# State-space block and routed experts: a convolution in three half-width products, and a drain in halves

## The reference, cut to what matters

```python
x = L0_attn_x                                       # (16, 512, 128), fp32
xn = layernorm(layernorm(x)) * norm_w + norm_b
x_in, z = split(xn @ in_proj_w.T)                    # 256 inner channels each
x_conv = conv(x_in, conv_w, taps=4, causal) + conv_b # full 256 x 256 x 4
x_act = silu(x_conv)
delta, B, C = x_act @ x_proj_w.T                     # 1 + 16 + 16
h = h * exp(-softplus(delta)) + B * x_act            # scan over 512 tokens
y = (h . C) * silu(z) @ out_proj_w.T + residual
x = x + layernorm(y)                                 # "third" norm
logits = layernorm(x) @ Wr + br                      # "fourth" norm
for e in 16 experts:                                 # top 2 of each token
    out += w_e * (layernorm((silu(x W1) * (x W3)) W2) * gamma + beta)
x = x + layernorm(out)
```

## Time and profile before

| | us |
|---|---|
| median of 3 runs | 971.87 (971.36 to 972.1) |
| the profiled execution, its own time | 974.93 |
| its span, first to last instruction | 973.1 |
| PE busy | 940.0 (97%) |
| DVE busy | 722.8 (74%) |
| ACT busy | 689.5 (71%) |
| POOL busy | 620.4 (64%) |

### The profile page before, as it was taken

The page is one execution under the profiler, slowest core; times in us unless marked ns, Lnnn a source line. Parts: engine busy times, 40 slices in busy tenths (PEclk is TensorE's granted clock), DMA queues, the critical chain, the costliest instruction groups (busy, mean ns, idle before and its releaser), DMA issues.

```text
span 973.1 us, 26657 instructions
## 1 busy us (share of the span) xinstructions
PE 940.0 (97%) x7207; PEld 833.9 (86%) x7207; DVE 722.8 (74%) x2524; ACT 689.5 (71%) x1358; POOL 620.4 (64%) x813
## 2 busy tenths in 40 slices
PE   8999999999999999998879999999999999999994
PEld 5777887788887887887879999999999999999951
DVE  2379999999999998898623767776767677677656
ACT  3777787777778778765115777777777778778536
POOL 2445777777778777775541666666666666566647
PEclk9999999999999999999988999999999999999997
DMA  4001323121111111110865211111111111111075
GB/s 136 12 12 34 93 93 97 58 62 48 55 56 53 53 43 42 42 42 22 324 238 175 87 44 51 49 51 46 49 50 48 47 50 49 42 53 50 18 293 225
DMA packets 54159, 75.25 MB, mean 77 GB/s; under 512 B 11103, under 2 KB 32865, under 8 KB 53376
## 3 DMA queue, kind: packets, MB, share of 16 engines
q1 hardware_dynamic: 42784, 54.87, 18.4%
q0 software_dynamic: 8672, 16.93, 4.8%
q10 hardware_dynamic: 2560, 1.75, 0.6%
HBM read 47.09 MB, written 27.41 MB: 77 GB/s over the span
## 4 chain that ended last, share of the span: by engine, by line
PE 79%; DVE 7%; POOL 6%; issue 5%; DMA 1%; ACT 1%; POOLq 0%; DVEq 0%; SPq 0%; ACTq 0%
PE pA L1886 11%; PE pR L1886 11%; PE pA L1472 11%; PE pB L1894 6%; PE pY L1894 5%; PE pY L1586 4%; PE pB L1498 3%; PE pB L1632 3%; PE pA L1487 3%; PE pY L1622 3%; PE pA L1443 3%; POOL chosen_scratch L656 2%; PE pY L1605 2%; PE pY L1554 2%; PE pR L1570 2%
## 5 line engine op out<-in xcount | busy, mean ns | idle before, releaser
L656 POOL DMA_INDIRECT chosen_scratch<-yo,got_id x143 | 146.8, 1027 | 93.7 <-issue 87.9
L961 ACT ACTIVATE stage<-w_sb 128x1024 f32 x143 | 151.2, 1057 | 55.7 <-issue 55.6
L1358 DVE TENSOR_TENSOR hidT<-pR,sil 128x512 f32<-128x512 f32 x143 | 98.9, 692 | 81.0 <-ACT sil L956 60.8
L595 POOL DMA_INDIRECT slots_scratch<-xrow,send_at x128 | 134.7, 1052 | 35.3 <-issue 31.3
L1886 PE MATMUL pA<-xsT,stage 128*128 128x128 f32 x1144 | 151.3, 275 | 0.4 <-ACT xsT L945 0.4
L1886 PE MATMUL pR<-xsT,stage 128*128 128x128 f32 x1144 | 151.1, 275 | 0.0
L1886 PEld LDWEIGHTS pA<-xsT,stage 128*128 128x128 f32 x1144 | 139.2, 192 | 0.7 <-ACT xsT L945 0.6
L1886 PEld LDWEIGHTS pR<-xsT,stage 128*128 128x128 f32 x1144 | 139.0, 192 | 0.0
L1472 PE MATMUL pA<-xn,taps 128*128 128x512 f32 x256 | 129.8, 594 | 1.0 <-ACT xn L722 1.0
L646 POOL TENSOR_TENSOR ers<-eve,neg_half 128x1 f32<-128x1 f32 x143 | 81.7, 571 | 57.2 <-DVE eve L1370 40.0
L956 ACT ACTIVATE sil<-pA 128x512 f32<-128x512 f32 x143 | 85.3, 596 | 26.5 <-PE pA L1886 21.7
(11 more groups left out here) (198 smaller groups left out, 2102.0 us busy)
## 6 DMA issues: line engine op xcount, KB each, us to landing
got<-slots_scratch SPq DMA_DIRECT2D x143, 65.0 KB, 1.9
w_sb<-chosen_scratch SPq DMA_DIRECT2D x16, 512.0 KB, 5.4
w_sb<-in_w_dram SPq DMA_DIRECT2D x1, 6144.0 KB
xin<-in_x_dram SPq DMA_DIRECT2D x16, 256.0 KB
xr<-in_x_dram SPq DMA_DIRECT2D x16, 256.0 KB, 3.1
x_scratch<-x SPq DMA_DIRECT2D x16, 256.0 KB
w_sb<-in_w_dram SPq DMA_DIRECT2D x4, 1024.0 KB, 7.2
fx<-x_scratch SPq DMA_DIRECT2D x1, 4096.0 KB
```

What stands on the lines that cost most here:

```text
L595: eng.indirect_dma_start(slots_d, bass.IndirectOffsetOnAxis(ap=send_at[:, s % 2, k, t:t + 1], axis=0), xrow[:, s % 2, k, t, :], None).then ...
L656: eng.indirect_dma_start(chosen_d, bass.IndirectOffsetOnAxis(ap=got_id[:, j % NGOT:j % NGOT + 1], axis=0), yo[:, q, :], None, bounds_check ...
L961: eng.activation(stage[:, j % NSTAGE, :, :].rearrange("p k f -> p (k f)"), w13_sb[:, bass.ds(e, 1), :, :].rearrange("p o k f -> p (o k f)" ...
L1358: eng.tensor_tensor(hidT[:, p, :], pR[:, p, :], sil[:, p, :], ALU.mult).then_inc(hid_ready, 1)
```

## The change

- The second 128 channels of the convolution (f = 1) are made by `fast_conv`: even and odd tokens share a product. Three products of 256 columns, each a sum of two weights, take the place of one of 512 columns with four: six matmuls of 256 columns for four of 512. Their inputs are every other column of `xn` and of its differences `xd` (POOL's new `differ`). `tapx` holds the sums and negatives of taps, made by DVE at the start. ACT copies the shared product (`shared_copy`, 256 columns), and DVE adds it to both halves (`join_taps`, 512 columns) before ACT's silu. The steps behind it wait for `cv_ready`.
- The epsilon of the third and fourth norm is added on POOL, not on DVE (`var_3` and `var_4` go). `shift_3` goes from every sequence; one operation makes all at the end. The copy of the indices in `choose` goes.
- `tail_at` is made inside the last `positions`. `conv`, `expand`, `fold`, the sends and the rest stand in new orders on all four engines, and loads of x stand one place earlier in SP's queue.
- The last sequence's output projection, norms and router are done in two halves of two tiles, in two banks. POOL sends one row between them and the other six after them, where it sent five ahead of them. The counts of `keep_warm` change.
- In stage 3 the negated mean goes, and the last group is normalised and added by DVE and stored by ACT.
- `load_middle` and `load_last`, which the diff also adds, are called nowhere.

The diff, cut to its core:

```diff
+FAST = (1,)
+SHARED = 256
...
+                for n, f in enumerate(FAST):
+                    even, odd = (taps[:, :, tile(f)].rearrange("p (k o) f -> p k o f", o=2)[:, :, o, :] for o in range(2))
+                    eng.tensor_tensor(tapx[:, n, 0:2, :], even, odd, ALU.add).then_inc(taps_ready, 1)
+                    eng.tensor_scalar(tapx[:, n, 2:4, :], odd, -1.0, None, ALU.mult).then_inc(taps_ready, 1)
...
+            def fast_conv(s, f, k):
+
+                n = FAST.index(f)
+                if k == 0:
+                    if n:
+                        need(eng, shared_ready, s, len(FAST), n)
+                    else:
+                        need(eng, prod_ready, s, 2, 2, ago=1)
+                else:
+                    need(eng, xd_ready, s, 1, 1)
+                half_seq = SEQ // 2
+                for q in range(2):
+                    if k == 0:
+                        out, h, src, at_col = pB[:, 1, SHARED:SHARED + half_seq], tapx[:, n, q, :], xn, 1 + 2 * q
+                    elif k == 1:
+                        out, h, src, at_col = pA[:, f, 0:half_seq], taps[:, 2 * q, tile(f)], xd, 2 * q
+                    else:
+                        out, h, src, at_col = pA[:, f, half_seq:SEQ], tapx[:, n, 2 + q, :], xd, 1 + 2 * q
+                    every_other = src[:, s % 2, at_col:at_col + SEQ].rearrange("p (i o) -> p i o", o=2)[:, :, 0]
+                    i = eng.matmul(out, h, every_other, start=q == 0, stop=q == 1)
+                if k == 0:
+                    i.then_inc(shared_mm, 1)
+                elif k == 2:
                     i.then_inc(cv_mm, 1)
...
+            def join_taps(s, f):
+
+                if s is None:
+                    return
+                n = FAST.index(f)
+                need(eng, cv_mm, s, 2, f + 1)
+                need(eng, shared_ready, s, len(FAST), n + 1)
+                need(eng, u_ready, s, 2, f + 1, ago=1)
+                eng.tensor_tensor(cvs[:, n, :].rearrange("p (i o) -> p i o", o=2), pA[:, f, :].rearrange("p (o i) -> p i o", o=2),
+                                  shared[:, :].rearrange("p (i o) -> p i o", o=1).broadcast_to([P, SEQ // 2, 2]), ALU.add).then_inc(cv_ready, 1)
...
+            def shared_copy(s, f):
+                if s is None:
+                    return
+                n = FAST.index(f)
+                need(eng, shared_mm, s, len(FAST), n + 1)
+                if n:
+                    need(eng, cv_ready, s, len(FAST), n)
+                else:
+                    need(eng, cv_ready, s, len(FAST), len(FAST), ago=1)
+                eng.activation(shared[:, :], pB[:, 1, SHARED:SHARED + SEQ // 2], ACT.Copy).then_inc(shared_ready, 1)
...
+            def differ(s):
+
+                if s is None:
+                    return
+                need(eng, xn_ready, s, 1, 1)
+                need(eng, cv_mm, s, 2, FAST[-1] + 1, ago=2)
+                eng.tensor_tensor(xd[:, s % 2, 0:SEQ + 2], xn[:, s % 2, 0:SEQ + 2], xn[:, s % 2, 1:SEQ + 3], ALU.subtract).then_inc(xd_ready, 1)
...
-                need(eng, moments3, s, 9, 9)
-                eng.tensor_tensor(rs3[:, :], ve3[:, :], neg_half[:, 0:NT4], ALU.pow).then_inc(rstd3, 1)
+                need(eng, moments3, s, 8, 8)
+                eng.tensor_tensor(ve3[:, :], mv3[:, s, :, 1:2].rearrange("p t o -> p (t o)"), eps[:, :], ALU.add).then_inc(rstd3, 1)
+                need(eng, rstd3, s, 2, 1)
+                eng.tensor_tensor(rs3[:, s, :], ve3[:, :], neg_half[:, 0:NT4], ALU.pow).then_inc(rstd3, 1)
...
-                need(eng, choice, s, 6, 4)
-                eng.tensor_copy(topi[:, :, :], topi8[:, :, 0:2].rearrange("p t k -> p k t")).then_inc(choice, 1)
-                need(eng, choice, s, 6, 5)
+                need(eng, choice, s, 5, 4)
                 eng.tensor_tensor(chosen[:, s % 2, :, :, :], iota_es[:, :].rearrange("p (a o e) -> p a o e", a=1, o=1).broadcast_to([P, 2, NT4, NE]),
-                                  topi[:, :, :].rearrange("p k (t o) -> p k t o", o=1).broadcast_to([P, 2, NT4, NE]), ALU.is_equal).then_inc(choice, 1)
...
+                if s == NS - 1:
+                    eng.wait_ge(rank_read, NS)
+                    eng.tensor_scalar(tail_at[:, :], running[:, :], slot_no[:, 0:1], None, ALU.add).then_inc(tail_ready, 1)
...
+            def rstd_half(moments, mv, ve, rs, done, h):
+                c = slice(2 * h, 2 * h + 2)
+                eng.wait_ge(moments, 8 * L + 4 + 4 * h)
+                eng.tensor_tensor(ve[:, c], mv[:, c, 1:2].rearrange("p t o -> p (t o)"), eps[:, c], ALU.add).then_inc(done, 1)
+                eng.wait_ge(done, 2 * (L + h) + 1)
+                eng.tensor_tensor(rs[:, c], ve[:, c], neg_half[:, c], ALU.pow).then_inc(done, 1)
...
+            address(L - 1)
+            send_ready(L - 1)
+            send_one(L - 1, 0, 0)
+            rstd_3_half(0)
+            rstd_3_half(1)
+            send_one(L - 1, 0, 1)
+            rstd_4_half(0)
+            rstd_4_half(1)
+            send(L - 1, 1)
+            send(L - 1, 2)
+            send(L - 1, 3)
+            token(L)
...
+            def attend_half(h):
+                eng.wait_ge(xr_loaded, 16 * NS)
+                eng.wait_ge(op_mm, L + 1 + h)
+                for t in half_tiles(h):
+                    i = eng.scalar_tensor_tensor(out=at[:, t, :], in0=xr[:, t, :], scalar=rs1[:, L, t:t + 1], in1=half_bank(h)[:, in_bank(t)], op0=ALU.mult, op1=ALU.add)
+                i.then_inc(at_ready, 1)
...
+            attend_half(0)
+            stats_half(at, at_ready, stats3, moments3, 0)
+            attend_half(1)
+            aggr_3_half(0)
+            stats_half(at, at_ready, stats3, moments3, 1)
+            aggr_3_half(1)
+            residual_half(0)
+            stats_half(x1, x1_ready, stats4, moments4, 0)
+            residual_half(1)
+            aggr_4_half(0)
+            stats_half(x1, x1_ready, stats4, moments4, 1)
+            aggr_4_half(1)
+            shift_4_half(0)
+            shift_4_half(1)
+            eng.scalar_tensor_tensor(out=shift3[:, :, :].rearrange("p s t -> p (s t)"), in0=mv3[:, :, :, 0:1].rearrange("p s t o -> p (s t o)"), scalar=-1.0,
+                                     in1=rs3[:, :, :].rearrange("p s t -> p (s t)"), op0=ALU.mult, op1=ALU.mult).then_inc(shift3_ready, 1)
+            logits_half(0)
+            largest_half(0)
+            where_half(0)
+            logits_half(1)
+            largest_half(1)
+            where_half(1)
+            choose(L)
+            margin(L)
+            positions(L)
...
+                from_state(q[5], 1)
+                bc_turn(q[4], 0)
+                project_gate(q[3], 1)
+                r_turn(q[4], 2)
+                diag_turn(q[4])
+                odd_turn(q[4])
+                x_turn(q[2])
+                project_state(q[3])
+                gram(q[4], 2)
+                gram(q[4], 4)
+                conv(q[2], 0, 0)
+                xf_turn(q[6])
+                delta_turn(q[3])
+                conv(q[2], 0, 1)
+                next_b(q[3])
+                route(q[6])
+                r_turn(q[4], 8)
+                conv(q[2], 0, 2)
+                r_turn(q[4], 4)
+                conv(q[2], 0, 3)
+                r16_turn(q[4], 0)
+                level(q[4], 2)
+                gram(q[4], 8)
+                project_gate(q[2], 0)
+                rank(q[6])
+                r16_turn(q[4], 1)
+                level(q[4], 8)
+                project_out(q[5])
+                level(q[4], 4)
+                states(q[4], 0)
+                conv(q[2], 1, 0)
+                states(q[4], 1)
+                conv(q[2], 1, 1)
+                h_turn(q[4], 0)
+                conv(q[2], 1, 2)
+                h_turn(q[4], 1)
+                from_state(q[4], 0)
...
+            def project_out_half(h):
+                eng.wait_ge(y_step, 11 * NS)
+                if h == 0:
+                    eng.wait_ge(rank_read, L)
+                else:
+                    eng.wait_ge(ht_ready, 2 * NS)
+                for t in half_tiles(h):
+                    for m in range(2):
+                        i = eng.matmul(half_bank(h)[:, in_bank(t)], y[:, m, tile(t)], outproj[:, m, :], start=m == 0, stop=m == 1)
+                i.then_inc(op_mm, 1)
...
             keep_warm(5)
-            project_out(15)
-            keep_warm(46)
-            xf_turn(15)
-            keep_warm(2)
-            route(15)
-            keep_warm(8)
-            rank(15)
-            keep_warm(16)
-            eng.wait_ge(lg_read, NS)
+            project_out_half(0)
+            project_out_half(1)
+            keep_warm(28)
+            xf_turn_half(0)
+            xf_turn_half(1)
+            route_half(0)
+            route_half(1)
+            keep_warm(10)
+            eng.wait_ge(lg_read, NS + 1)
+            rank(L)
...
-            keep_warm(50)
+            keep_warm(40)
...
-            keep_warm(48)
+            keep_warm(57)
...
```

(93 more changed lines are left out.)

479 lines of the change are left out of this document (267 added, 212 removed).

## The result

The changed kernel is slower: 995.58 us median (992.59 to 996.9) against 971.99 (971.36 to 975.96) for the kernel before, a ratio of 1.0239 with an interval of 1.0218 to 1.0259. The forecast was 950.9, in a range of 942 to 963. The profiled execution took 995.67 us, span 993.9.

The account below looks back on a forecast made before the run. PE was taken to bound steady stage 1, with DVE close behind and a serial chain of waits between the stages. Terms -0.7 - 6.8 - 0.8 - 11 - 1.7 = -21.0 took 971.87 to 950.9 us, range 942 to 963.

Parts of the forecast that it names:

- DVE's own need stays at 26.2: Steady stage 1: DVE's added and removed operations net to 0 (-0.1 to +0.2), leaving its need at 26.2 us a unit.
- The steady term: Steady stage 1: the unit falls from 27.22 to 26.7 us over 13 units, -6.8 us (bounds -11.2 and 0).
- POOL holds DVE: Rival, steady stage 1: `differ` holds DVE for its whole 1.33 us, +4.9 for -6.8, 962.6 us; chance 0.07.
- half speed: Rival, steady stage 1: reading every other column halves PE's speed, +22.4 over 13 units, 980.1 us; chance 0.05.
- PE alone: Steady stage 1: PE by itself would need 27.22 - 0.86 = 26.36 us a unit.
- the tie at 26.7: Steady stage 1: PE waits 0.35 us before `diag_turn` for DVE's fold, making the unit 26.7 us.
- The start: Before the first `project_state`: one shortened convolution, against 0.3 to 0.5 us of making `tapx`; -0.7 us (+1 to -2).
- The last two units: End of stage 1, no convolution: DVE sets the pace and loses 0.66 less some waits; -0.8 us (0 to -1.5).
- Between the stages: From last projection to stage 2's first tile: earlier rank and ten fewer useless products; -11 us (-5 to -13.5).
- P: Start of the last sequence's projection, 475.16 us in the kernel before; later steps between the stages are counted from it.
- Stage 3: Negated mean removed, -0.5, and the last group's end moved to DVE, -1.2; together -1.7 us (-0.7 to -2.5).

Follow-up runs that it names:

- e2: Changed kernel with one POOL line moved, `address` ahead of `carry(.,1)` and `join(.,1)`, all work kept: 969.27 us, 0.9934 of the kernel before.
- e6: On e2, DVE's `dots` moved ahead of `stats_1` and `with_diagonal` behind `largest`, no work changed: 964.83 us, 0.992 of the kernel before.
- e14: On e6, POOL's difference made for the first two units only, so the output is not the reference's: 964.75 us, 0.9945 of the kernel before.
- The probes: Behind e6's last output, single DVE operations started beside two POOL operations (products, copies or tiny copies), with or without a wait between; no run time given.
- e12: Kernel before with `address` moved behind `join(.,1)` on POOL and `positions` behind `aggr_1` on DVE: 1010.58 us, ratio 1.0384.
- e9: On e6, the loads of `gamma` and `beta` (2 MB) issued behind the stores of the tails: 967.61 us, 0.9911 of the kernel before.
- e13: Changed kernel with `address` between `carry(.,1)` and `join(.,1)` on POOL: 984.72 us in one execution.
- e3: Changed kernel, same order, second 128 channels again by four full products, without DVE's sum and ACT's copy: 995.41 us, 1.0216 of the kernel before.
- e8: On e2, the load of experts 4 to 14 issued earlier, at `ys_mm`: 973.96 us, 1.0011 of the kernel before.

## Why the prediction was wrong

**The step that failed** is the cost of the new order of steady stage 1: "DVE's own need stays at 26.2". I counted the operations that the change adds and takes, each at its old length, and took the new order for a matter of waits only. But an operation's length depends on what POOL does at that time. Three unchanged operations grew by some 4.0 us a unit: 26.2 + 4.0 is 30.2, near the 29.7 measured, and DVE became the bound. The steady term, -6.8 for 13 units, came out at 372.9 - 353.8 = +19.1. e2 and e6 show that the order alone makes the difference.

**The rival was the right mechanism in the wrong place.** "POOL holds DVE" had 0.07, and was priced as the length of the new operation, `differ`, 1.33 a unit. `differ` costs nothing (e14, in e6's order). The holder is POOL's old `carry(.,1)` and `join(.,1)`, 2.5 us back to back, which the order moved beside `placed`; the sign of it (`var_4`, which "ended when POOL's product did") was in front of me. Priced by the longest run of POOL's products, 2.5 us, the rival is 26.2 + 2.5 = 28.7 a unit, 13 x 1.5 = +19 against -14 elsewhere: on the slower side. The argument "most of DVE's operations keep their length beside POOL's" was true of the old order, which says nothing of a new one. The Trainium skill, SBUF — State Buffer, section Who interferes with whom, has the rule: a VectorE operation in a two-port mode, or with two SBUF inputs while GpSimd's reads SBUF, and GpSimd's own exclude one another, and the later stands still until the first is done. The probes agree (0.29 to 1.33 us, and 0.29 to 0.29 with PSUM), and so does e12, where the hold ends with one instruction. The 3.27 us of `placed` reach over two, which that rule does not give (see Open).

**Right:** the products. PE's timeline in the changed kernel has two shares of the convolution, each two products of 256 columns in four instructions:

```profile
225.70 1.07 PE L1701 MATMUL pA<-xd,taps 128*128 128x256 f32 x4
...
228.36 1.08 PE L1701 MATMUL pA<-xd,tapx 128*128 128x256 f32 x4
229.28 0.63 PE L1848 MATMUL pR<-ident,Hs 128*128 128x128 f32 x4
```

From 228.36 to 229.28 two products cost 0.92 us, 0.46 each, where 0.43 was put, and "half speed" is refuted. Six of them for four of 0.86 save 0.7 us, so PE alone needs 26.5 a unit; with the hold away the unit is 26.57, where PE alone was put at 26.36 and the tie at 26.7. e6's 13 units from fold 0 to 13 give 345.5 for 353.8 us: -8.3 where -6.8 stood, 1.3 of it from unit 1 alone, which no term of the forecast has. The tie at `diag_turn` was not seen. `join_taps` took 0.68 as put.

**The start** cost 4.6 us for -0.7: fold 0 at 60.90. Of it 1.7 are an inner weight that landed later in this execution and a lower clock (the first product 5.29 us for 3.70; e6 has 3.70 and fold 0 at 59.15). The rest, 2.9, shows in e2 and e6 too, and the forecast has no term for it: between 18 and 32 us of e6 PE waits three times, 2.7 us together, for ACT's `zs`, where the kernel before waits 0.8 us for ACT. What else is in it was not followed. Unit 1 gives 1.4 back (25.6 us).

**The last two units** cost 56.5 us in the changed kernel and 54.7 in e6, for 52.85 before: +1.9 by themselves where -0.8 stood. The trace shows where the 1.9 are: the unit from fold 13 to 14 takes 28.4 us in both (26.3 before). PE stands idle in it for ACT's decays, at a wait that the new order puts ahead of `route(12)` and the old one behind `gram(14, 8)`:

```profile
442.94 0.71 PE L1646 MATMUL pA<-ident 128*128 128x128 f32 x4 [2.98 <-ACT dec L836]
```

Behind this idle time the granted clock fell to the lower level (0.50 from 416 to 418 us in e6, 0.51 from 446 to 448 in the changed kernel); in the same place the kernel before has PE busy for 12.96 of 13 us at clock 1.00. No run moved the wait. The rest of the changed kernel's 3.7, its last unit of 28.1 us for 26.6, is open.

**Between the stages** the chain did what it was to do and the time did not follow. PE, then SP's queue:

```profile
502.67 1.06 PE L2061 MATMUL pB<-outproj,y_both 128*128 128x128 f32 x8
...
516.87 0.20 PE L1891 MATMUL pB<-chosen_b,ones_b 128*128 128x80 bf16 x1
540.80 0.45 PE L2106 MATMUL pB<-ident,got 128*128 128x128 f32 x1 [8.71 <-DMA got<-slots_scratch]
541.61 2.07 PE L2114 MATMUL pA<-xsT,stage 128*128 128x128 f32 x8 [0.37 <-ACT xsT L1043]
```

```profile
519.15 9.98 SPq L332 DMA_DIRECT2D slots_scratch<-blank  x8
538.85 8.08 SPq L497 DMA_DIRECT2D got<-slots_scratch  x8
```

The rank came at P+14.2 (P+12.6 forecast, P+21.7 before; a send that stalled 1.09 us is most of the 1.6), `tail_at` at once behind it, the projection at full clock. But the first tile came at P+38.1, not P+34 to 36: -8 for -11. The tails were issued in 9.98 us, and 9.7 us pass from there to the first slot's load, where the kernel before has 2.5: SP waits 2.2 us for the store of x and then 6.5 for the tails. By the pages' medians one of SP's tails takes 8.3 us from issue to landing, 2.9 in the kernel before. It is issued beside the weights' transfer, whose last part, `beta`, lands at 528.7 (25.9 behind its issue). Bounded by the transfers, the gap no longer follows the rank: in four kernels the first slot's load stands 36.5 to 37.4 behind the weights' issue. PE ran out of useless products and stood idle for 8.71 us; its granted clock was 0.50 from 538 to 547 us (1.2 of 2.4 GHz), the first eight products of stage 2 took 2.07 for 1.16, and stage 2 was 2.5 us longer (401.5 for 399.0). I had named both ("the weights' load still runs", "a PE that waits for the slot may start stage 2 at the lower clock") and given them 2 us (-11 for -13); they took 5 in the gap and 2.5 in stage 2. e9 shows that the 2 MB behind the weights are not it; whether the sends or the weights' own 6 MB end last was not separated.

**Stage 3:** from the last product of stage 2 to the end 51.6 for 52.9 us: -1.3 for -1.7, right.

**The sum**, by the profiled spans (us; forecast, changed kernel, e6 with the hold away):

| stretch | forecast | changed | e6 |
|---|---|---|---|
| start to first fold 0 | -0.7 | +4.6 | +2.9 |
| folds 0 to 13 | -6.8 | +19.1 | -8.3 |
| folds 13 to 15 | -0.8 | +3.7 | +1.9 |
| fold 15 to first tile of stage 2 | -11 | -7.9 | -7.4 |
| stage 2 | 0 | +2.5 | +1.6 |
| stage 3 | -1.7 | -1.3 | -0.7 |
| sum | -21.0 | +20.7 | -10.0 |

e6 is 7.3 us faster than the kernel before by the medians of its comparison (964.83 for 972.12): without the hold the sign of the forecast is right, and its size was missed by start, last units and gap.

**Open:** in the changed kernel `placed` starts, by the records, 0.41 us into one of POOL's sends and 0.6 us ahead of `carry`, and ends behind `join` (behind `carry` in e13, where `join` does not follow). Where it starts with `carry` running, it ends with `carry`, although `join` follows at once: so in e12, in the probes, and in one unit of e3 (DVE, then POOL):

```profile
421.79 1.55 DVE L1373 TENSOR_TENSOR placed<-chosen,place 128x128 f32<-128x128 f32 x1
```

```profile
421.68 1.51 POOL L580 TENSOR_TENSOR R<-u,dec 128x512 f32<-128x512 f32 x1 [2.21 <-PE pR L1832]
423.16 1.08 POOL L603 TENSOR_TENSOR dec<-dec 128x512 f32<-128x512 f32 x1
```

The send alone does not hold it: in e2 `placed` starts at the same 0.41 us into a send, with `carry` not behind it, and takes 0.29 us. Nor does the contact always hold: it took 0.28 us in one unit of nine of the changed kernel, and in the three units of e3 where it started 0.44 to 0.66 us into the send. What part the send has in the longer hold, and what decides between the two, no run separated.

## What to carry to other kernels

When an order is changed, lay the queues of DVE and GpSimd side by side at their new times before costing anything: each pair of a GpSimd product and a DVE operation that touches SBUF alone can cost up to the rest of GpSimd's run, here up to 3 us for an operation of 0.28. Place GpSimd's long products beside DVE operations with a PSUM input, statistics or reductions, and a wait that is there anyway (here `address`) can be the fence. When a chain is shortened, look for what ends just behind it: here transfers kept some 3 of the 11 us that the chain should have given.

## What the runs showed of the hardware

- DVE operations with fp32 SBUF operands alone, one input or two, copy and constant forms too, are held by a GpSimd product: 0.29 to 1.33, 0.23 to 1.27, 0.43 to 1.47 us. With a PSUM input, `bn_stats` and reduce: not held. Beside GpSimd copies of 128x512 (two in 1.28 us) the same forms take 0.66, 0.60 and 0.80 us.
- The hold goes the other way too: the power of eight elements took 2.68 us on POOL in the changed kernel, behind `carry(.,8)` and beside DVE's `with_diagonal`, and 1.67 in e6.
- A product that reads every other fp32 column of SBUF costs PE by its 256 columns, 0.46 us, where 512 adjacent ones cost 0.86.
- A GpSimd indirect store stood at its issue while the weights were on their way: 8.14 us in e8, 1.09 in the changed kernel.
